# One-hot products for the first and last expert slot, a query stage in two groups, and four score buffers in the second attention

## What is computed

```python
x = x + causal_attention(layernorm(x), ctx, ctx)              # 16 heads of 32
x = x + experts(layernorm(x), gate_w, w1, w2, w3)             # 8 experts, top 2 of them per row
x = x + quantized_attention(layernorm(x), ctx, Wq, Wkv, Wp)   # q, k, v and the weights rounded to 8 bits
x = x + ternary_feed_forward(layernorm(x), ...)               # three ternary weight matrices
```

```python
probs = softmax(x @ gate_w.T); topk_w, topk_idx = top_k(probs, 2); topk_w /= sum(topk_w)
y_e = (silu(x @ w1[e]) * (x @ w3[e])) @ w2[e]                 # out = sum over the row's two experts of topk_w * y_e
q = quantize((x @ Wq + bq) / sqrt(32))                        # per row and head: round(q / s), s = max|q| / 127
attn = softmax(q @ k.T); attn = round(attn / s8) * s8; out = attn @ v
```

## Time and profile before

| | |
|---|---|
| profiled execution | 1674.77 us |
| its span, first to last instruction | 1672.7 us |
| median of three runs | 1672.83 us |
| PE (TensorE) busy | 1411.1 us (84%) |
| DVE (VectorE) busy | 1008.1 us (60%) |
| ACT (ScalarE) busy | 765.9 us (46%) |
| POOL (GpSimd) busy | 435.3 us (26%) |
| chain of waits | PE 49%, DVE 22%, issue 13%, DMA 7%, ACT 5%, POOL 2% |
| mean granted TensorE clock | 0.838 of full |

### The profile page before, as it was taken

How to read it: one execution, slowest core, us unless ns; L and a number is a source line. 1 busy time by engine, 2 the same in 40 slices (tenths; PEclk the granted TensorE clock), 3 DMA queues, 4 the chain that set the end, 5 groups by cost and what they waited for, 6 DMA issues and landing times.

```text
span 1672.7 us, 23161 instructions
## 1 busy us (share of the span) xinstructions
PE 1411.1 (84%) x8009; PEld 680.8 (41%) x8056; DVE 1008.1 (60%) x1669; ACT 765.9 (46%) x1095; POOL 435.3 (26%) x323
## 2 busy tenths in 40 slices
PE   7993888888743999999999999186888888878878
PEld 3441555555441444444444444142333333324334
DVE  5998999999850111111011111576999999974895
ACT  4774888888710010111001100136777777762553
POOL 1115000000005678999900000321111111110341
PEclk9996999999956999999999999595555555559989
DMA  7997565555109999999988887528999999993001
GB/s 248 266 291 172 108 118 128 127 115 107 39 4 363 401 362 390 372 402 397 399 321 299 302 298 187 169 58 160 197 217 212 217 214 218 209 204 82 1 0 51
DMA packets 494197, 352.27 MB, mean 211 GB/s; under 512 B 407224, under 2 KB 409272, under 8 KB 493504
## 3 DMA queue, kind: packets, MB, share of 16 engines
q1 hardware_dynamic: 479344, 302.06, 67.3%
q0 software_dynamic: 10816, 40.90, 7.5%
q10 hardware_dynamic: 3984, 8.65, 1.4%
HBM read 206.32 MB, written 38.27 MB: 146 GB/s over the span
## 4 chain that ended last, share of the span: by engine, by line
PE 49%; DVE 22%; issue 13%; DMA 7%; ACT 5%; POOL 2%; DVEq 0%; POOLq 0%; SPq 0%; ACTq 0%
PE scores L930 19%; PE bank L946 10%; DVE arena L1669 7%; DMA arena<-arena 5%; PE bank L846 4%; PE bank L830 2%; DVE arena L1490 2%; ACT arena L1272 2%; DVE arena L1476 2%; PE bank L829 2%; ACT arena L1212 2%; PE bank L938 1%; PE bank L1117 1%; PE bank L975 1%; POOL arena L717 1%
## 5 line engine op out<-in xcount | busy, mean ns | idle before, releaser
L1669 DVE TENSOR_SCALAR_CACHE_REDUCE arena<-scores,arena 128x1024 f32<-128x1024 f32 x256 | 318.4, 1281 | 33.7 <-ACT arena L1272 16.1
L930 PE MATMUL scores<-arena 128*128 128x512 f32 x736 | 322.3, 596 | 0.8 <-DVE arena L1606 0.8
L991 PE MATMUL scores<-arena 96*128 96x512 bf16 x512 | 263.8, 621 | 51.5 <-DVE arena L1669 40.0
L1272 ACT ACTIVATE arena<-arena 128x2048 int16<-128x2048 f32 x128 | 256.2, 2002 | 100.5 <-POOL arena L731 81.5
L1614 DVE TENSOR_TENSOR arena<-scores,arena 128x512 f32<-128x512 f32 x46 | 31.8, 691 | 447.9 <-PE scores L930 447.9
L930 PEld LDWEIGHTS scores<-arena 128*128 128x128 f32 x736 | 140.8, 191 | 178.3 <-issue 177.1
L946 PE MATMUL bank<-arena 128*128 128x512 f32 x368 | 163.4, 597 | 3.5 <-issue 3.3
L1240 ACT ACTIVATE arena<-scores 128x512 f32<-128x512 f32 x46 | 27.5, 597 | 249.4 <-PE scores L930 249.4
L1476 DVE TENSOR_REDUCE arena<-scores 128x1 f32<-128x640 f32 (+3 forms) x128 | 127.7, 1018 | 8.1 <-PE scores L807 7.7
L1212 ACT ACTIVATE arena<-bank 128x512 f32<-128x512 f32 (+3 forms) x256 | 116.6, 506 | 26.0 <-PE bank L830 26.0
L1490 DVE TENSOR_TENSOR arena<-arena 128x1024 f16<-128x1024 f32 (+2 forms) x128 | 126.1, 1026 | 3.5 <-issue 1.8
(11 more groups left out here) (239 smaller groups left out, 2041.2 us busy)
## 6 DMA issues: line engine op xcount, KB each, us to landing
arena<-in_L_ffn_w SPq DMA_DIRECT2D x69, 2048.0 KB, 12.6
arena<-arena SPq DMA_DIRECT2D x32, 256.0 KB, 3.0
kst_d<-arena POOLq DMA_DIRECT2D x16, 384.0 KB, 6.4
tern_d<-arena POOLq DMA_DIRECT2D x12, 512.0 KB, 6.9
arena<-kst_d SPq DMA_DIRECT2D x16, 384.0 KB, 4.2
xs_d<-arena SPq DMA_DIRECT2D x23, 256.0 KB, 3.5
arena<-xs_d SPq DMA_DIRECT2D x23, 256.0 KB, 13.7
ys_d<-arena ACTq DMA_DIRECT2D x23, 256.0 KB, 7.1
```

Source lines behind the costliest of these rows:

```text
L930: ins = pe.matmul(scores[:, m * 1024 + half * 512:m * 1024 + half * 512 + 512], xsT[a][:, c], wa[:, m, c, half * 512:half * 512 + 512], st ...
L991: ins = pe.matmul(scores[:, s:s + 512], qhead[a][0:K3, t * P:(t + 1) * P], khead[a][0:K3, s:s + 512], start=True, stop=True)
L1272: act.activation(p16[t % PBUF], ssb[i], ACT.Exp, bias=ebias[i], scale=-1.0, accum_out=rsum[a][:, t:t + 1]).then_inc(p_ready, 1)
L1669: dve.tensor_scalar(ssb[i][:, s:s + 1024], scores[:, s:s + 1024], nsq[:, bass.ds(h, 1), t], None, ALU.mult, ALU.min, accum_out=nmx[i][:, h ...
```

## The change

1. *First slot.* Its rows are no longer read back from DRAM. VectorE builds a one-hot matrix per row tile (`oh0`: does this row's first or second position equal column p?), and TensorE makes the turned slot by 32 products `xn` x `oh0` summed over tiles. The expert numbers of the slots (slot_e) are computed seven steps earlier, and SP starts at step 29. The rows of slot 1 still come from `xs_d`; their load now stands behind the weight loads of slots 0 and 1. `xs_d` is still filled by 16 scatters.
2. *Last slot.* Its y is not stored. VectorE builds a weighted one-hot matrix (`ohl`), TensorE turns it, ScalarE copies it (`ohT`), and after the last slot eight products `ohT` x y write their share for all rows into the eight PSUM banks. The gathers (of posg, with positions of the last slot masked to 0 and their weights too) wait only for the slots up to 21. VectorE adds the gathered rows, then the eight banks.
3. *Query stage in two groups.* The norm is computed for tiles 0 to 3 and then 4 to 7; the rows are normalized on ScalarE. Wq and its bias are loaded ahead of the two transposes of the feed-forward weights. The q rows are turned by DMA transposes from SP and stored as the keys are. The keys of heads 0 and 1 are loaded early; Wp and its bias are loaded right before the attention loop.
4. *Four score buffers.* `ssb`, the minima and the biases are four deep; the two new buffers lie over Wq and over the q rows.

```diff
-            sp.wait_ge(r_step, R_STEPS)
+            sp.wait_ge(r_step, R_SLOTS)
...
                     if past(u, 2):
                         sp.wait_ge(xs_turned, at(u - 2))
-                    if not first:
                         sp.dma_start(xsin[a], xs_d[bass.ds(u * P, P), :]).then_inc(xs_loaded[a], 16)
...
-                    if first:
+                    if not first and not past(u, 2):
 
                         sp.wait_ge(scattered, 16 * 2 * NT)
                         sp.dma_start(xsin[a], xs_d[bass.ds(u * P, P), :]).then_inc(xs_loaded[a], 16)
...
+            sp.dma_start(wq_sb, Wq.rearrange("(k p) n -> p k n", p=P)).then_inc(wq_loaded, 16)
+            sp.dma_start(bq_row, bq.partition_broadcast(P)).then_inc(wq_loaded, 16)
             for w in range(2):
                 sp.dma_start_transpose(wT[w].rearrange("p o c n -> p (o c) n"), tern_d[w]).then_inc(wT_in, 16)
...
+            sp.wait_ge(moe_added, 3 * NT)
+            load_keys(0)
+            load_keys(1)
+            for u in range(NT):
+                sp.wait_ge(q3_ready, u + 1)
+                if u >= 2:
+                    sp.wait_ge(qst_stored[u % 2], 16 * (u // 2))
+                sp.dma_start_transpose(qTbuf[u % 2], q3row[u % 2].rearrange("p h c d -> p (h c d)")).then_inc(kT_in[u % 2], 16)
+            for a in range(2):
+                sp.wait_ge(qst_stored[a], 16 * (NT // 2))
+            load_queries(0)
+            load_queries(1)
             sp.dma_start(wp_sb, ...)
...
             pool.wait_ge(scattered, 16 * 2 * NT)
+            pool.wait_ge(xs_turned, 1)
+            pool.wait_ge(oh_turned, 2)
...
-            for a, m in ((0, (SLOTS + 1) // 2), (1, SLOTS // 2)):
-                pool.wait_ge(y_stored[a], 16 * m)
+            for a in range(2):
+                pool.wait_ge(y_stored[a], 16 * (SLOTS // 2))
...
             for u in range(NT):
-                pool.wait_ge(qT_ready, 2 * u + 2)
-                pool.dma_start(qst_d[:, :, u * P:(u + 1) * P].rearrange("h r n -> r h n"), qTbuf[u % 2][0:K3]).then_inc(qst_stored[u % 2], 16)
+                pool.wait_ge(kT_in[u % 2], 16 * (NC // 2 + u // 2 + 1))
+                pool.dma_start(q_rows[:, :, u * P:(u + 1) * P], qTbuf[u % 2]).then_inc(qst_stored[u % 2], 16)
...
+            for t in range(NT):
+                pe.wait_ge(r_step, R_STEPS + NT + t + 1)
+                for c in range(KC):
+                    ins = pe.matmul(bank6[:, c * P:(c + 1) * P], xn[:, t, c * P:(c + 1) * P], oh0[:, t], start=t == 0 and c == 0,
+                                    stop=t == NT - 1 and c == KC - 1, skip_group_check=True)
+            ins.then_inc(xs_turned, 1)
+            pe.wait_ge(r_step, R_LAST)
+            for g, bank in enumerate((bank4, bank5)):
+                for t in range(4):
+                    ins = pe.transpose(bank[:, t * P:(t + 1) * P], ohl[:, 4 * g + t], idf)
+                ins.then_inc(oh_turned, 1)
...
+            for t in range(NT):
+                pe.matmul(last_bank(t), ohT[:, t * P:(t + 1) * P], yb[(SLOTS - 1) % 2], start=True, stop=True).then_inc(last_done, 1)
...
+            for t in range(QT):
+                turn_x(t)
+            pe.wait_ge(wq_loaded, 32)
             project_q(0)
-            for u in range(NT):
-                if u + 1 < NT:
-                    project_q(u + 1)
-                turn_q(u, u % 2, u == 0)
+            project_q(1)
+            for t in range(QT, NT):
+                turn_x(t)
+            for u in range(2, NT):
+                project_q(u)
...
+            for t in range(NT):
+                dve.tensor_scalar(oh0[:, t], iota_p, r1[0][:, t:t + 1], None, ALU.is_equal).then_inc(r_step, 1)
+            for t in range(NT):
+                dve.wait_ge(r_step, R_STEPS + t + 1)
+                dve.scalar_tensor_tensor(oh0[:, t], iota_p, r1[1][:, t:t + 1], oh0[:, t], ALU.is_equal, ALU.add).then_inc(r_step, 1)
+            n = R_FIRST
+            for j in range(2):
+                r(dve.scalar_tensor_tensor(wm[j], r1[j], LAST_AT, r1[8 + j], ALU.is_lt, ALU.mult))
+                r(dve.scalar_tensor_tensor(posm[j], r1[j], LAST_AT, r1[j], ALU.is_lt, ALU.mult))
+                r(dve.tensor_copy(posg[:, j], posm[j]))
+                r(dve.tensor_scalar(posl[j], r1[j], -LAST_AT, None, ALU.add))
+            for t in range(NT):
+                for j, dst in enumerate((ohl, ohl2)):
+                    dve.tensor_scalar(dst[:, t], iota_p, posl[j][:, t:t + 1], r1[8 + j][:, t:t + 1], ALU.is_equal, ALU.mult).then_inc(r_step, 1)
+            r(dve.tensor_tensor(ohl, ohl, ohl2, ALU.add))
...
+            for g in range(2):
+                gs = slice(g * GT, (g + 1) * GT)
+                for t in range(g * GT, (g + 1) * GT):
+                    dve.wait_ge(last_done, t + 1)
+                    dve.tensor_tensor(xres[:, t], last_bank(t), xres[:, t], ALU.add).then_inc(moe_added, 1)
+                    tile_stats(2, t)
...
...
                 if u >= 2:
-                    dve.wait_ge(q3_turned, 2 * (u - 1))
+                    dve.wait_ge(kT_in[a], 16 * (NC // 2 + u // 2))
...
+            for g in range(2):
+                root(3 + g, std0[:, half(g)], ln_t[:, 0, half(g)])
+                act.wait_ge(q_step, 6 * (g + 1))
+                for t in range(g * GT, (g + 1) * GT):
+                    act.activation(xn3[:, t], xres[:, t], ACT.Identity, scale=ln_t[:, 1, t:t + 1], bias=ln_t[:, 5, t:t + 1]).then_inc(x3_ready, 1)
+                for t in range(g * GT, (g + 1) * GT):
+                    act.wait_ge(x3_turned, t + 1)
+                    act.activation(XT3[:, :, t * P:(t + 1) * P], scores[...], ACT.Copy).then_inc(x3T_ready, 1)
...
-                i, n = t % 2, 8 * h + t
-                if not (first and t < 2):
-                    dve.wait_ge(p_ready, n - 1)
+                i, n = t % SBUFS, 8 * h + t
+                if not (first and t < SBUFS):
+                    dve.wait_ge(p_ready, n - SBUFS + 1)
```

More of the change, by code:

```diff
@@ L183, in program @@
         iota_s = keep.take(F32, SLOTS + 1)
+        iota_p = keep.take(F32, P)
         stats = keep.take(F32, NT, 6)
@@ L261, in program @@
         rm = Region(base)
-        wbuf = [(rm.take(F32, 2, KC, EH), rm.take(F32, EC, D)) for _ in range(2)]
+        wbuf = [(rm.take(F32, 2, KC, EH), rm.take(F32, EC, D))]
+        wbuf1_at = rm.at
+        wbuf.append((rm.take(F32, 2, KC, EH), rm.take(F32, EC, D)))
         xsin = [rm.take(F32, D) for _ in range(2)]
@@ L272, in program @@
         vinv = rm.take(F32, D)
+        ohT = rm.take(F32, T)
+        posg = rm.take(I32, 2, NT)
+        wm, posm, posl = ([rm.take(F32, NT) for _ in range(2)] for _ in range(3))
         m_mark = rm.at
         xn = rm.take(F32, NT, D)
+        over_XT = Region(rm.at)
+        oh0, ohl, ohl2 = (over_XT.take(F32, NT, P) for _ in range(3))
         XT = rm.take(F32, KC, T)
@@ L308, in program @@
         nsq = rq.take(F32, H, NT)
+        over_q3 = Region(rq.at)
         q3row = [rq.take(BF16, H, 3, HD) for _ in range(2)]
-        qTbuf = [rq.take(BF16, H, P) for _ in range(2)]
+        qTbuf = [rq.take(BF16, 3 * HD * H // P, P) for _ in range(2)]
+        over_q3.end = rq.at
         khead = [rq.take(BF16, B * SK) for _ in range(2)]
@@ L314, in program @@
         ssb = [rq.take(F32, B * SK) for _ in range(2)]
-        nmx = [rq.take(F32, 2) for _ in range(2)]
-        ebias = [rq.take(F32, 1) for _ in range(2)]
+        nmx = [rq.take(F32, 2) for _ in range(SBUFS)]
+        ebias = [rq.take(F32, 1) for _ in range(SBUFS)]
         over_xn3 = Region(xn3_at, xn3_at + 4 * NT * D)
@@ L954, in _ @@
             pe.wait_ge(y_ready, SLOTS)
-            turn_rows(pe, xn3, ln_step, LN_STEPS * 3 - NT, x3_turned, x3T_ready, (bank4, bank5), idf)
-            def turn_q(u, a, first):
-                pe.wait_ge(q3_ready, at(u))
-                if not first:
-                    pe.wait_ge(qT_ready, 2 * u)
-                for g, bank in enumerate((bank4, bank5)):
-                    view = bank[:].bitcast(BF16)
-                    for h in range(8):
-                        ins = pe.transpose(view[0:K3, h * P:(h + 1) * P],
-                                           q3row[a][:, 8 * g + h].rearrange("p c d -> p (c d)"), idb)
-                    ins.then_inc(q3_turned, 1)
@@ L968, in _ @@
[L968 to L982 removed]
+            pe.wait_ge(xsT_ready, SLOTS)
@@ new lines, in _, with turn_x @@
+            pe.wait_ge(h_done, 2 * SLOTS)
+            for t in range(NT):
+                pe.matmul(last_bank(t), ohT[:, t * P:(t + 1) * P], yb[(SLOTS - 1) % 2], start=True, stop=True).then_inc(last_done, 1)
+            def turn_x(t):
+                pe.wait_ge(x3_ready, t + 1)
+                if t >= 2:
+                    pe.wait_ge(x3T_ready, t - 1)
+                for c in range(KC):
+                    ins = pe.transpose(scores[:, (t % 2) * 512 + c * P:(t % 2) * 512 + (c + 1) * P], xn3[:, t, c * P:(c + 1) * P], idf)
+                ins.then_inc(x3_turned, 1)
@@ new lines, in project_q @@
+            def project_q(u):
```

(10 more changed lines are left out.)

172 lines of the change are left out of this document (91 added, 81 removed).

## The result

The changed kernel takes 1655.29 us (median of four runs, 1654.15 to 1657.65) against 1673.44 us for the kernel before (four runs, 1671.62 to 1675.98): a ratio of 0.9897, 95% interval 0.9885 to 0.991, or 17 to 18 us less. The forecast was 1651.8 us with a range of 1638 to 1667. The profiled execution took 1657.65 us, its span 1655.9.

The account below looks back on a forecast made before the run. TensorE was taken to bound the expert stage, a chain of waits the handover, and SP's transpose queue with its DMAs the second attention. Savings of 3 + 16.5 + 1.5 = 21 us from 1672.8 gave 1651.8 us, range 1638 to 1667.

Parts of the forecast that it names:

- First slot: Front of the expert stage: slot 0 starts about 521.5 instead of 528.2, slot 1 at 550 instead of 553.4; 3 us.
- Last slot: Handover after the expert stage: gathers start at 1031, the last lands at 1055; 16.5 us together with the query stage.
- Query stage: Before the second attention: VectorE decides at 4.0 us a tile, first score read near 1124.3; 16.5 us with the last slot.
- the ring: Two-buffer round of DMA transpose and store for query rows: 8.1 us per two tiles, just keeping up with VectorE.
- a quiet stage: Query stage: the ground for taking the keys' minimum transfer times, giving a ring round of 8.1 us.
- Four buffers: Second attention: of 16.1 us of VectorE's waits for ScalarE only 1.5 us gained, bounds 0 and 12.
- the sum of SP's issue times: Second attention: a head's transposes and two loads take SP 21.9 us, with no hole in its queue.
- The handover: From the expert stage's last store to the first score read: last slot and query stage together, 16.5 us, bounds 0 and 22.
- the front did not pay in full: Rival at the expert stage's front: slot 1's rows arrive in time, 9 us instead of 3, kernel 1646; chance 0.11.
- the 14.9 at which it would have made the kernel slower: Rival in the query stage: the ring decides from a 14.9 us round; at 17, 8.4 us slower, 1681; chance 0.06.

## Why the prediction was right, and where it was not

The median lies 3.5 us above the forecast of 1651.8, inside the range. The path ran where the forecast had put it. That the total is so near is in part luck, since single terms erred both ways.

**First slot: 3 forecast, 2.4 measured** by the distance from the first scatter (2.5 by the run that undoes it). The account held. The one-hot product took 9.65 us, not 15, and slot 0 started at 516.60, not 521.5, set by its weights. Slot 1's load landed at 541 as forecast (539 to 543). What I left out was the clock: in the 9 us of waiting it fell, and from the turn to slot 1's start it took 11.4 us instead of the 8.8 that I had carried over, 1.7 of this in the down products. The pair of profiled executions shows 1.4, of which 0.8 are lost since the changed one reaches its first scatter that much later.

**Last slot.** In brackets the forecast on the clock of before, with slot 1 at 553.4; it started at 552.72. First gather 1031.63 (1031), last landing 1055.3 (1055), adds done 1058.3 (1058), group 0 at 1066.4 (1066), group 1 at 1074.4 (1074): each step came out within 1.5 us. But I never asked what the step is worth in this order of work, and the run without it answers 4 us at most. All 16 gather adds stand ahead of the first statistics, so group 0 waits for rows it does not need. The run that sorts the adds by group gets 3.4 to 4.4 us out of that.

**Query stage: the step that was mis-sized is the ring.** Counted from slot 1's start, the first read of a query projection was forecast 15.6 us earlier than in the earlier trace rows, and came 15.8 earlier. From there to the first score read I had 47.3 us; it took 50.8. I put the round of transpose and store at 8.1 us, from the fastest of the keys' transfers; it took 10.9 in the mean, between their fastest (3.6 + 4.2) and their middle values (6.2 + 6.4). With four buffers the same stretch takes 45.4 us. My reason for the minima (a quiet stage) did not hold. The transpose of one tile runs beside the store of the other; that this slows them was not tested alone. Last slot and query stage together gave 13.2 us instead of 16.5.

The Trainium skill, VectorE: DVE Perf Modes, "The three transpose paths", with its 1309 ns for a 128x128 block by DMA, was set against the keys' transfers. The query transposes on the chain above, 12 blocks each, landed after 3.65 to 6.33 us, so it does not hold here either.

**Four buffers: 1.5 forecast, 2.6 measured** (not clear of nothing, hardly over 5), inside the bounds of 0 and 12. The mechanism is shown, the size is not: the transposes' DMA traffic sets the beat; with half of it the buffers are worth 7.1 us. I had priced it by the sum of SP's issue times; taking the loads from SP's queue did not make the loop faster and left the engines' share as it was, so it is the DMA engines, and SP's durations follow them. The rest of the loop's 4.4 us in this pair of profiles is not shown to be the buffers': in the nine profiles with four buffers and this loop it took 351.5 to 354.4 us, in the one with two buffers 353.9. The Trainium skill, DMA: Bandwidth & Descriptors, "Latency and other measured facts", gives DMA transposes 261 GB/s where a middle dimension is not contiguous, and about 350 to 400 where it is. This loop moved 212 with its loads, and the 128 transposes of 512 KB alone 189 by the same 355 us, so it does not reach either.

**The sum:** 3 + 16.5 + 1.5 = 21 were forecast. The two spans show 0.7 + 13.2 + 4.4 less 1.4 behind the loop, which is 16.8 with rounding; the medians 18.1. The handover's miss of 3.3 us is the ring: 3.5 there, 0.2 the other way ahead of it. The first slot came out 0.6 short by the distance and 2.3 by the two spans, and the loop gave 2.9 more than forecast. The rivals: the front did not pay in full, but would have with the load elsewhere in the queue (8.4 us, where I had 6 more); the ring held the query stage up, by 5.4 us against the four-deep one, and its round of 10.9 stayed below the 14.9 at which it would have made the kernel slower.

## What to carry to other kernels

When a change frees the first item of a pipeline, look at what the second one waits for, and where its request stands in its queue: here one load of 256 KB behind 10 MB gave back four fifths of the gain, and moving one line brought 8 us. A ring of DMA transfers should not be priced by the fastest of its nearest relatives: 8.1 us by them, 12.6 by their medians, 10.9 measured. The test is to deepen it. Before adding buffers ahead of a saturated transfer, halve the transfer once: the difference between deep and shallow buffers then shows how much the transfer hides. And a part of a change that looks worth little in one order of work can be worth more in another: the last slot's products gave 4 us at most as written, and 8.7 with the adds sorted.

## What the runs showed of the hardware

After a wait of 9.09 us between fp32 products at full clock TensorE came back at the low one (granted 0.50 from 538 to 547 us; a turn of four blocks 1.12 us instead of 0.66, and 16 down products 8.78 instead of 7.10); after a wait of 1.06 or 3.39 us it kept the full clock. A load of 256 KB landed 12.6 us after its issue when it stood behind five loads of 2 MB in the same queue, 4.9 us when it stood behind four, the last of which SP had begun to issue 28 us and finished issuing 15 us ahead, and 7.0 us from another engine's queue beside six. A loop of DMA transposes from SBUF to SBUF with its loads moved 212 GB/s, while the expert stage, mostly loads of 2 MB, moved 350. The loads of a head, given a queue of their own, did not raise that (211 GB/s; 103.6% and 10.1% of the engines for the two queues, 112.5% for one before), and the longest wait for a landing on TensorE went from 2.8 to 4.2 us. Halving the bytes of a transpose brought its landing from 4.7 to 3.1 us in the median, and the time that SP's queue shows for it from 2.38 to 1.23.
